# Masked scores ahead of k and of the output's split, and the first SiLU ahead of probabilities, in the mixed slots of an attention and feed-forward kernel

## The reference

```python
x = x + _layernorm(_L0_attn_ref(_layernorm(x), w_qkv, b_qkv, w_out, b_out))
x = x + _layernorm(_L0_ffn_ref(_layernorm(x), gate_w, up_w, down_w, gate_scale, up_scale, down_scale))

# attention, per head and chunk of 128
inter = einsum('bhcd,bhde->bhce', qb * decay_q, S)
scores = einsum('bhcd,bhed->bhce', qb, kb) * dmask
intra = einsum('bhce,bhed->bhcd', scores, vb)
S_new = lam_c * S + einsum('bhcd,bhce->bhde', kb * decay_k, vb)
out = inter + intra
# feed-forward
gate = silu(quantized_matmul(x, gate_w, gate_scale))
fuse = gate * quantized_matmul(x, up_w, up_scale)
y = quantized_matmul(fuse, down_w, down_scale)
```

## Time and profile before

| what | value |
|---|---|
| time, median of 3 runs | 988.04 us (987.9 to 988.89) |
| profiled execution, its own time | 988.57 us |
| its span | 986.8 us |
| TensorE matmul busy | 958.7 us, 97% |
| VectorE busy | 690.4 us, 70% |
| GpSimd busy | 687.6 us, 70% |
| ScalarE busy | 509.1 us, 52% |

### The profile page before, as it was taken

The page is one execution under the profiler, slowest core; times in us unless marked ns, Lnnn a source line. Parts: engine busy times, 40 slices in busy tenths (PEclk is TensorE's granted clock), DMA queues, the critical chain, the costliest instruction groups (busy, mean ns, idle before and its releaser), DMA issues.

```text
span 986.8 us, 22045 instructions
## 1 busy us (share of the span) xinstructions
PE 958.7 (97%) x8498; PEld 708.9 (72%) x8498; DVE 690.4 (70%) x1359; ACT 509.1 (52%) x985; POOL 687.6 (70%) x837
## 2 busy tenths in 40 slices
PE   8999999999998999999999999999999999999996
PEld 6777777786766777767677676767767676776764
DVE  7999998875887675767667576766757676665422
ACT  3656665565654544636354463635446363544522
POOL 2699998986775675849567584947758594775733
PEclk9999999999999999999999999999999999999999
DMA  9899899999983983847658284766828476512200
GB/s 322 210 290 265 255 276 293 277 254 297 229 207 88 202 180 56 196 93 163 131 127 176 61 194 94 163 128 129 191 48 193 92 165 125 127 52 43 41 26 22
DMA packets 297642, 159.88 MB, mean 162 GB/s; under 512 B 141632, under 2 KB 272832, under 8 KB 297408
## 3 DMA queue, kind: packets, MB, share of 16 engines
q1 hardware_dynamic: 296672, 157.86, 67.4%
q10 hardware_dynamic: 864, 0.61, 0.2%
HBM read 82.93 MB, written 41.94 MB: 127 GB/s over the span
## 4 chain that ended last, share of the span: by engine, by line
PE 57%; DVE 17%; POOL 11%; issue 10%; ACT 4%; DMA 1%; POOLq 0%; DVEq 0%; SPq 0%; ACTq 0%
PE bank L892 17%; PE bank L874 12%; PE bank L767 8%; PE att L767 7%; PE bank L782 7%; POOL att_pool L1059 4%; DVE stats L1326 3%; DVE p L1367 3%; DVE state_hl L1397 3%; DVE w_pool L1460 2%; POOL rstd L998 2%; ACT w_pool L596 2%; POOL w_pool L1077 2%; PE att L851 1%; DVE state L1386 1%
## 5 line engine op out<-in xcount | busy, mean ns | idle before, releaser
L874 PE MATMUL bank<-f_pool,gate_q 128*128 128x256 f16 x1536 | 185.0, 274 | 4.3 <-ACT w_pool L596 3.8
L874 PE MATMUL bank<-f_pool,up_q 128*128 128x256 f16 x1536 | 183.7, 273 | 1.5
L892 PE MATMUL bank<-down_q,w_pool 128*128 128x512 f16 x768 | 168.3, 379 | 0.0
L874 PEld LDWEIGHTS bank<-f_pool,gate_q 128*128 128x128 f16 x1536 | 147.4, 98 | 27.0 <-ACT w_pool L596 6.5
L874 PEld LDWEIGHTS bank<-f_pool,up_q 128*128 128x128 f16 x1536 | 149.4, 98 | 22.4 <-DVE w_pool L1460 5.1
L1059 POOL TENSOR_TENSOR att_pool<-p,att_pool 128x512 f16<-128x512 f32 x128 | 145.7, 1159 | 28.0 <-ACT att_pool L548 27.9
L1460 DVE SCALAR_TENSOR_TENSOR w_pool<-bank,us_t,w_pool 128x256 f32<-128x256 f32 x192 | 84.1, 479 | 112.5 <-ACT w_pool L596 54.7
L995 POOL TENSOR_TENSOR rstd<-mv,eps_t 128x1 f32<-128x1 f32 (+1 forms) x112 | 30.1, 269 | 181.3 <-DVE mv L1329 181.3
L892 PEld LDWEIGHTS bank<-down_q,w_pool 128*128 128x128 f16 x768 | 74.0, 98 | 86.9
L1077 POOL TENSOR_TENSOR w_pool<-w_pool 128x512 f16<-128x512 f32 x96 | 111.3, 1165 | 28.0 <-ACT w_pool L602 27.9
L548 ACT CAST att_pool<-p 128x512 f16<-128x512 f32 x128 | 75.7, 615 | 62.4 <-DVE p L1367 62.3
(11 more groups left out here) (145 smaller groups left out, 1826.4 us busy)
## 6 DMA issues: line engine op xcount, KB each, us to landing
xr<-in_x SPq DMA_DIRECT2D x32, 512.0 KB, 4.6
dram_qk<-qk_hl SPq DMA_DIRECT2D x64, 256.0 KB, 3.7
att_pool<-dram_qk SPq DMA_DIRECT2D x64, 256.0 KB, 5.3
f_pool<-dram_qk SPq DMA_DIRECT2D x64, 256.0 KB, 5.6
dram_kd<-kd_hl SPq DMA_DIRECT2D x32, 256.0 KB, 2.9
dram_v<-vv SPq DMA_DIRECT2D x32, 256.0 KB, 3.7
qn_pool<-dram_qk SPq DMA_DIRECT2D x32, 256.0 KB, 6.2
out_x<-w_pool SPq DMA_DIRECT2D x32, 256.0 KB, 2.3
```

Source lines behind the costliest of these rows:

```text
L874: ins = nc.tensor.matmul(b[:, j * TOK:(j + 1) * TOK], w[:, k, o * P:(o + 1) * P], x1_hl[:, v % 2, part, k], start=(k == 0 and part == 0), ...
L892: ins = nc.tensor.matmul((b_gate, b_up)[t][:, :], h_hl[:, part, k, t * P:(t + 1) * P], down_q[:, k], start=(k == 0 and part == 0), stop=(k ...
```

## The change

TensorE's, GpSimd's and SP's lists stay as they are. On VectorE, in first_slot masked(0, 1, 0) comes before k_lo(14, 2). In second_slot masked(1, 1, 0) comes before k_lo(15, 3), masked(1, 1, 1) before out_sum(1, 0), o_max(1, 0) before state_lo(1, 1), and masked(2, 0, 0) is taken out of slot(2) and put between scale_o(1) and o_lo(1). In slot(2) product(0, 0) comes before carry_and_state(2, 0). On ScalarE, in slot(2), silu(0, 0) comes before probs_hi(2, 0, 0). No instruction is added or removed.

```diff
@@ScalarE, slot(s)
-                if attends:
+                if s == 2:
+                    silu(v, 0)
                     probs_hi(s, 0, 0)
-                silu(v, 0)
+                else:
+                    if attends:
+                        probs_hi(s, 0, 0)
+                    silu(v, 0)
                 if attends:
                     state_hi(s, 0)
@@VectorE, first_slot
                 state_lo(0, 0)
+                masked(0, 1, 0)
                 k_lo(LEAD, 2)
-                masked(0, 1, 0)
                 out_sum(0, 0)
@@VectorE, second_slot
                 x1_moments(0, 1)
+                masked(1, 1, 0)
                 k_lo(n, 3)
-                masked(1, 1, 0)
+                masked(1, 1, 1)
                 out_sum(1, 0)
-                masked(1, 1, 1)
                 v_sum(n, 0)
                 carry_and_state(1, 1)
                 v_sum(n, 1)
+                o_max(1, 0)
                 state_lo(1, 1)
-                o_max(1, 0)
                 out_sum(1, 1)
                 o_max(1, 1)
                 scale_o(1, slice(0, T), 3)
+                masked(2, 0, 0)
                 o_lo(1)
@@VectorE, slot(s)
-                if attends:
-                    masked(s, 0, 0)
+                if s == 2:
+                    product(v, 0)
                     carry_and_state(s, 0)
-                product(v, 0)
-                if v >= 1:
-                    y2_moments(v - 1, 1)
+                else:
+                    if attends:
+                        masked(s, 0, 0)
+                        carry_and_state(s, 0)
+                    product(v, 0)
+                    if v >= 1:
+                        y2_moments(v - 1, 1)
```

## The result

The changed kernel takes 990.44 us (median of 10 runs, 989.83 to 991.02), against 988.0 us (10 runs, 987.63 to 988.89) for the kernel before: a ratio of 1.0023, 95% interval 1.0013 to 1.0032. It is slower by 2.4 us. The profiled execution took 990.63 us with a span of 988.8; the one of before took 988.57 and 986.8.

What follows compares the result with a forecast made beforehand. TensorE, busy 97% of the span, was taken as the bound, with GpSimd's gapless 26 us block limiting gains. -0.75 at attend(2, 1) plus 1.65 for one clock fall gave +0.90 on 988.57: 989.5, range 987.0 to 991.0.

Steps and rivals of the forecast that it cites:

- one fall of the clock: TensorE's clock drops once around the new pauses, ahead of gate_up(0, 0) in the sum: +1.65, total 989.5, chance 0.41.
- rival 2: Slower: two clock falls, one at each new pause; attend(2, 1) 2.3 us later, 990.9, chance 0.22.
- First slot: masked(0, 1, 0) ahead of k_lo(14, 2) on VectorE: everything after comes 0.60 us earlier (bounds 0.2 and 0.62).
- The masked scores of the second slot: Masked scores ahead of k_lo(15, 3) and out_sum(1, 0): carry of unit 2 +1.34, pause ahead of attend(1, 1) 2.3.
- The turn: Into slot(2), silu(0, 0) and product(0, 0) earlier: gate_up(0, 1) on TensorE -1.59, the state's update +0.62.
- GpSimd's block: GpSimd's gapless 26 us from h_lo(0, 0): 0.61 later, holding TensorE to -0.75 at attend(2, 1), 2.5 pause before gate_up(0, 3).
- The clock: New TensorE pauses before the carry of unit 2 and gate_up(0, 3): one fall likelier than none, costing 0 to about 2 us.
- Rival 1: No fall of TensorE's clock: -0.75, 987.8; no fall (987.8 to 988.0) has chance 0.27.
- Rival 3: Faster: GpSimd's block doesn't bind, TensorE keeps 2.2 us: 986.4, chance 0.07.
- Rival 4: Change does nothing; old waits and old fall stood beside GpSimd's block: 988.0; no fall (987.8 to 988.0) has chance 0.27.

Runs made afterwards that it cites:

- The part alone: Kernel before with only masked(1, 1, 0) ahead of k_lo(15, 3) and masked(1, 1, 1) ahead of out_sum(1, 0): 989.75 us against 988.43.
- three fillers: Changed kernel with extra unread matmuls in TensorE's pauses ahead of attend(1, 1), the carry of unit 2 and gate_up(0, 3): 988.18 us against 988.2 before.
- two fillers: Changed kernel with 12 extra unread matmuls ahead of attend(1, 1) and 18 ahead of the carry of unit 2: 988.87 us against 988.2 before.
- the change without the second slot's masked scores: Changed kernel without that part, GpSimd's kd_lo and v_lo of unit 15 moved to the end of slot(2): 984.94 us, ratio 0.9965 to the kernel before.
- the splits late: Kernel before with only GpSimd's kd_lo and v_lo of unit 15 moved to the end of slot(2): 986.61 us against 988.12.
- out_sum ahead and the splits late: Changed kernel, out_sum(1, 0) again ahead of masked(1, 1, 1), GpSimd's kd_lo and v_lo of unit 15 at slot(2)'s end: 986.0 us against 988.43 before.

## Why the prediction was right

The time lies in the range, and nearly all terms of the sum came out. But the forecast was one fall of the clock, 989.5, no change that a measurement can tell; what came is rival 2, two falls, worked out at 990.9, and the measured 990.44 is just over the bound of 0.2%. That it lies in the range is owed to a range drawn wide enough for the rival, not to the forecast.

- **First slot.** Forecast -0.60, measured -0.72 at carry(1, 0) and -0.75 at attend(1, 1). k_lo(14, 3) has no wait any more, and project_v(14, 0) waits 0.96 for the later k_lo(14, 2), and starts 0.24 earlier than before, where 0.2 was worked out.
- **The masked scores of the second slot.** The pause ahead of attend(1, 1) was put at 2.3; it is 2.29. The carry of unit 2 was to be 1.34 late, less the first slot's 0.60: +0.74. Measured +0.57. The part alone lost 1.30 at the carry and 1.3 in the time.
- **The turn.** For gate_up(0, 1) the working gives -0.60 - 1.59 + 1.65 for the fall = -0.54; measured -0.80, and with the clock held by fillers -2.42, against -2.19.
- **GpSimd's block.** It ends 1.25 later, where +0.61 - 0.60 + 1.65 = 1.66 was worked out for one fall. Without a fall +0.01 was worked out, and with three fillers it ends 0.13 earlier. The pause ahead of gate_up(0, 3) was to be 2.5, and is 2.31; a part of TensorE's wait for the block is already taken ahead of attend(2, 0), which the prediction left out. That the block binds there is shown by the kernels in which it is shorter: the pause shrinks to 0.39 and 0.55.
- **The clock.** This is the step that was mis-weighed. The place of both falls was in the prediction, but two falls had a chance of 0.22. I took the 5 us of full work around the third pause as speaking against a fall; that did not keep it away. The first fall's price was right, 1.77 us in the medians where 1.65 was expected. The second's was put at 1.7 and is 0.69. On TensorE it did take 1.7 (5.17 us from gate_up(0, 3) to the scores behind it, instead of 3.49), but at attend(2, 1) only 1.08 of it is seen, since without the fall 0.6 goes to the wait for the masked scores. Besides, some executions may not have it: four of the 11 runs with two fillers took 988.14 or less at a granted clock of 0.997 or 0.998, the others 988.81 or more at 0.995 to 0.997.
- **Rival 1** (no fall, 987.8 to 988.0) is what the kernel with three fillers shows, 988.18. The Trainium skill's rule (TensorE: Matmul & The Clock Gate, HAM oscillation) warns of single gaps longer than any here, and by it no fall was due; it is not borne out, since both falls followed pauses of 2.3 us or less.
- **Rival 3** (GpSimd doesn't bind) is out. **Rival 4**, that the gain stood beside GpSimd's block all along, is half of the story: with the falls taken away the change is worth nothing that the times tell (988.18 against 988.2), and with the block short the change without the second slot's masked scores is worth 1.7 us (984.94 against 986.61).

What stays open: the rule by which the clock falls. The runs show only that a pause of 1.54 with one of 0.81 behind it did it in some executions (987.4 with the splits late, 985.8 with the turn and the first slot's move too) and not in others, and that a pause of 2.3 did it in the trace of after and not in that of 984.7. The spread of 3 us of the kernel with out_sum ahead and the splits late is open too. The even 0.35 us that the later slots give back was not looked into. That the second slot's first step, masked(1, 1, 0) ahead of k_lo(15, 3), lengthens the pause by 0.8 and brings nothing is read from traces; it was not run alone.

## What to carry to other kernels

Before an instruction is moved ahead of another, ask whether it waits for an engine at that place: an operation that had been filling this wait then stands behind it. Here that alone put the carry 1.3 us back, and the time by 2.5 together with a clock that stayed low until 303.9 instead of about 300. Time that an early TensorE wins is worth nothing as long as the next engine's block of work has no gap; find that block first and shorten it, and most of the same reordering pays. Pauses of TensorE have a second price besides their length, the clock after them, and where they can't be removed, matmuls that nobody reads can hold it: they took back the 2.4 us here.

## What the hardware showed

- TensorE's clock fell to its lower level (0.50 granted, 1.2 GHz) after a pause of 2.3 us between long stretches of full work, and stayed down across a further pause (297.1 to 303.9 us). The two falls cost 1.8 and 0.7 us of the time. With idle matmuls in the three pauses the clock stayed at 1.00. In another execution (984.7) a pause of 2.31 us left it at 1.00 without any.
- The same order of instructions had its fall at different places in different executions: at 307.7 in the trace of before, at 300.4 with the splits late.
- A VectorE instruction on 128x2 values took 1.07 us instead of 0.17 beside a GpSimd instruction of 1.14, and the state's low half 2.04 instead of 1.17. Not every instruction is held up: the three of 0.69 us between these two, out_sum's and o_max's, took the same 0.69 beside kd_lo and v_lo.
